# Delta-attention layer on one core: one VectorE multiply scales the a and q rows of a level, the query norm is folded into the output norm, and the queues are reordered

## What is computed

```python
q = _conv_silu(x @ Wq, conv_q).reshape(b, t, H, DH)
k = _conv_silu(x @ Wk, conv_k).reshape(b, t, H, DH)
v = _conv_silu(x @ Wv, conv_v).reshape(b, t, H, DH)
g_raw = (x @ Wfa @ Wfb).reshape(b, t, H, DH) + dt_bias.reshape(H, DH)
g = -jnp.exp(A_log)[None, None, :, None] * _softplus_stable(g_raw)
beta = jax.nn.sigmoid(x @ Wb)
qf = _l2norm(q) * DH ** (-0.5)
kf = _l2norm(k)
def step(state, inp):
    q_i, k_i, v_i, g_i, b_i = inp
    state = state * jnp.exp(g_i)[..., None]
    inner = jnp.einsum('bhk,bhkv->bhv', k_i, state)
    state = state + jnp.einsum('bhk,bhv->bhkv', b_i[..., None] * k_i, v_i - inner)
    o_i = jnp.einsum('bhk,bhkv->bhv', q_i, state)
    return (state, o_i)
...
rstd = jax.lax.rsqrt(jnp.mean(o * o, axis=-1, keepdims=True) + EPS)
o = o * rstd * norm_w * jax.nn.sigmoid(g_out)
return o.reshape(b, t, KD) @ Wo
```

## Time and profile before

| | |
|---|---|
| median of three runs | 6265.92 us |
| lowest and highest of them | 6243.98 and 6275.91 us |
| the profiled execution | 6272.03 us |
| its span, first to last instruction | 6270.3 us |
| the 32 passes in it | 2168 to 4352 us |
| TensorE's granted clock, whole span | 0.939 |
| TensorE's granted clock in the passes | 0.99 |

### The profile page before, as it was taken

How to read it: one execution, slowest core, us unless ns; L and a number is a source line. 1 busy time by engine, 2 the same in 40 slices (tenths; PEclk the granted TensorE clock), 3 DMA queues, 4 the chain that set the end, 5 groups by cost and what they waited for, 6 DMA issues and landing times. The chain is left out here.

```text
span 6270.3 us, 125078 instructions
## 1 busy us (share of the span) xinstructions
PE 5487.5 (88%) x53008; PEld 3632.2 (58%) x53008; DVE 3220.0 (51%) x4649; ACT 2789.8 (44%) x5107; POOL 2304.6 (37%) x1583
## 2 busy tenths in 40 slices
PE   6888699755999599989989989998999988889999
PEld 5777466543666266666666666665444456664444
DVE  5555444434444376776776677675212166552221
ACT  3233444454444456555655655665211166662111
POOL 4554100001000176777777677675222200002222
PEclk8999799877999799999999999999999988889999
DMA  0000100000000000000000000000211100002111
GB/s 29 3 2 2 33 1 1 16 0 33 1 1 3 22 17 23 18 17 23 18 17 17 24 17 17 23 18 9 107 40 40 34 11 0 0 1 108 39 40 46
DMA packets 60618, 137.02 MB, mean 22 GB/s; under 512 B 11638, under 2 KB 24054, under 8 KB 58842
## 3 DMA queue, kind: packets, MB, share of 16 engines
q1 hardware_dynamic: 60122, 129.79, 6.2%
HBM read 127.26 MB, written 2.50 MB: 21 GB/s over the span
## 5 line engine op out<-in xcount | busy, mean ns | idle before, releaser
L607 PE MATMUL ps<-moe_xn_all,moe_w 128*128 128x512 f32 x1792 | 810.5, 595 | 0.0
L720 DVE TENSOR_TENSOR moe_h<-moe_silu,ps 128x512 f32<-128x512 f32 x224 | 153.9, 687 | 936.2 <-ACT moe_silu L662 929.1
L607 PEld LDWEIGHTS ps<-moe_xn_all,moe_w 128*128 128x128 f32 x1792 | 341.2, 191 | 424.1 <-issue 423.5
L662 ACT ACTIVATE moe_silu<-ps 128x512 f32<-128x512 f32 x224 | 133.8, 597 | 986.5 <-PE ps L607 986.4
L1797 DVE SCALAR_TENSOR_TENSOR kda_cv<-kda_pre,kda_w_front,kda_cv 128x1024 f32<-128x1024 f32 x297 | 554.8, 1885 | 1.3
L563 POOL TENSOR_TENSOR moe_h<-moe_h,moe_cb 128x512 f32<-128x512 f32 x176 | 233.6, 1327 | 696.4 <-DVE moe_h L720 696.4
L1983 POOL TENSOR_TENSOR kda_g<-kda_g,kda_f 128x512 f32<-128x512 f32 x225 | 395.4, 1757 | 205.7 <-DVE kda_rows L1975 197.1
L617 PE MATMUL ps<-moe_h,moe_w 128*128 128x512 f32 x896 | 420.4, 592 | 0.0
L1681 PE MATMUL ps<-kda_xn_all,kda_w_front 128*128 128x512 f32 x808 | 373.6, 606 | 26.0 <-DMA kda_w_front<-in_Kw 23.5
L1975 POOL TENSOR_TENSOR kda_rows<-kda_q,kda_f 128x512 f32<-128x512 f32 x225 | 361.1, 1605 | 16.6 <-POOL kda_f L1984 1.6
L1984 POOL TENSOR_TENSOR kda_f<-kda_f 128x512 f32<-128x512 f32 x225 | 313.9, 1395 | 17.6
(11 more groups left out here) (505 smaller groups left out, 12513.3 us busy)
## 6 DMA issues: line engine op xcount, KB each, us to landing
kda_col<-kda_beta SPq DMA_DIRECT2D x34, 512.0 KB, 3.9
moe_w<-in_Mw SPq DMA_DIRECT2D x6, 2816.0 KB, 19.6
moe_cb<-kda_beta SPq DMA_DIRECT2D x64, 256.0 KB, 3.1
kda_w_front<-in_Kw SPq DMA_DIRECT2D x34, 455.0 KB, 4.7
moe_cb<-kda_beta SPq DMA_DIRECT2D x32, 224.0 KB, 2.9
kda_w_out<-in_Kw SPq DMA_DIRECT2D x32, 192.5 KB, 2.4
moe_cb<-kda_beta SPq DMA_DIRECT2D x32, 192.0 KB, 2.8
moe_cb<-kda_beta SPq DMA_DIRECT2D x32, 160.0 KB, 2.7
```

Source lines behind the costliest of these rows:

```text
L607: last = nc.tensor.matmul(ps_gu[u % 2][r], w13[:, k, i, r], n.xn[:, k, cols(c)], start=k == 0, stop=k == KD - 1)
```

## The change

It does the following.

- `q` and `a` lie in one tile `aq_rows`, and `scale_both` multiplies both halves by `f` in one VectorE instruction of 1024 elements for levels 1 to 6. GpSimd's q instruction of those levels goes. Level 0 stays on GpSimd.
- `widen` is cut in two: GpSimd widens the columns before it waits for the rows, and the rows behind that wait.
- The query is no longer normalised: `squares(0)`, `log_sum(0)`, `root(0)` and `q_row` go. ScalarE squares q into `q_sq` instead (`q_square`), and VectorE adds it, scaled, to the squares of the output (`with_query`), ahead of the tail's `square_sums`.
- TensorE does `scores(l + 1)` right behind `lt_times_t(l)`, ahead of `t_times_x(l)`; `values` moves from level 4 to behind level 5.
- On ScalarE and VectorE front and tail pieces are put at other places; the first tap of the next front (`first_tap`) is done at the end of a pass instead of behind its first rows.
- A table that nothing reads (`level_mask`, 128 by 448 floats) is no longer loaded at the start of the launch. `lt6` shares the memory of `z`.

```diff
-            def squares(i):
-                if i == 0:
-                    pe.wait_ge(m.vt_in_sb, at(m.vt_in_sb, 1))
-                else:
-                    pe.wait_ge(m.ss_read, at(m.ss_read, 1))
-                pe.wait_ge(m.sq_ready, at(m.sq_ready, i + 1))
+            def squares():
+                pe.wait_ge(m.proj_read, at(m.proj_read, 2))
+                pe.wait_ge(m.sq_ready, at(m.sq_ready, 1))
...
+            def q_square():
+                act.wait_ge(m.silu_ready, at(m.silu_ready, 1))
+                if in_chain:
+                    act.wait_ge(m.ysum_ready, at(m.ysum_ready, 1))
+                nc.scalar.activation(o.q_sq[:], o.q[:], ACT.Square).then_inc(m.qsq_ready, 1)
...
-            def q_row():
-                dve.wait_ge(m.rs_ready, at(m.rs_ready, 1))
-                nc.vector.scalar_tensor_tensor(o.q[:], o.q[:], float(KDA_HEAD) ** -0.5, t2[:], ALU.mult,
-                                               ALU.mult).then_inc(m.rows_ready, 1)
...
+            def with_query():
+                dve.wait_ge(n.ysq, at(n.ysq, 2))
+                if turn.index:
+                    dve.wait_ge(m.qsq_ready, at(m.qsq_ready, -1))
+                nc.vector.scalar_tensor_tensor(y_sq[:], o.q_sq[:], QUERY_EPS * KDA_HEAD, y_sq[:], ALU.mult,
+                                               ALU.add).then_inc(m.ysum_ready, 1)
...
+        def scale_both(o, l, done):
+            h = 1 << l
+            blocks = [P, 2, UNITS * SEQ // (2 * h), h]
+            out = rows_s[l % 2][:].rearrange("p r u (b h) -> p r (u b) h", h=h)
+            src = o.aq[:].rearrange("p r u (b two h) -> p r (u b) two h", two=2, h=h)[:, :, :, 1]
+            decay = halves(o.f[:], h, 1).unsqueeze(1).to_broadcast(blocks)
+            nc.vector.tensor_tensor(out, src, decay, ALU.mult).then_inc(done, 1)
...
         def first_rows(pool, step, o):
...
-            pool.wait_ge(m.rows_ready, at(m.rows_ready, 2))
-            for r in range(2):
-                scale_rows(nc.gpsimd, o, 0, r, n.first_scaled)
+            pool.wait_ge(m.rows_ready, at(m.rows_ready, 1))
+            scale_rows(nc.gpsimd, o, 0, 0, n.first_scaled)
             pool.wait_ge(n.g_clear, at(n.g_clear, 1))
+            widen_columns(step, o, 0)
+            pool.wait_ge(m.silu_ready, at(m.silu_ready, 3))
+            scale_rows(nc.gpsimd, o, 0, 1, n.first_scaled)
             pool.wait_ge(n.first_scaled, at(n.first_scaled, 2))
-            widen(step, o, 0)
+            widen_rows(step, o, 0)
...
-                scale_rows(nc.gpsimd, cur, l, 1, n.scaled)
                 nc.gpsimd.tensor_tensor(halves(cols_s[l % 2][:], h, 0), halves(cur.col[:], h, 0),
                                         halves(decay_g[:], h, 0), ALU.mult).then_inc(n.scaled, 1)
-                pool.wait_ge(n.scaled, at(n.scaled, 2 * l))
+                pool.wait_ge(n.scaled, at(n.scaled, l))
+                widen_columns(step, cur, l)
                 pool.wait_ge(n.rows_scaled, at(n.rows_scaled, l))
-                widen(step, cur, l)
+                widen_rows(step, cur, l)
...
+            lt_times_t(4)
+            scores(5)
+            t_times_x(4)
+            tail.y_of(1)
+            f.squares()
+            lt_times_t(5)
+            last_scores()
+            t_times_x(5)
+            f.values()
+            tail.square_sums()
             last_x()
-            pe.wait_ge(m.ss_read, at(m.ss_read, 2))
+            pe.wait_ge(m.vt_in_sb, at(m.vt_in_sb, 1))
             ahead.project(0)
```

More of the change, by code:

```diff
@@ L1847, in column @@
                                                ALU.mult).then_inc(m.rows_ready, 1)
-            return Calls(clip=clip, tap=tap, corr=corr, q_row=q_row, a_row=a_row, column=column)
+            return Calls(clip=clip, tap=tap, corr=corr, a_row=a_row, column=column)
         def tail_pe(pe, o, w, quad):
@@ L1968, in residual @@
                 nc.vector.tensor_tensor(xs, two(OUT[k]), xs, ALU.add).then_inc(n.x_done, 1)
[L1970 removed]
+            return Calls(inner=inner, right_side=right_side, gate=gate, with_query=with_query, scale=scale,
+                         residual=residual)
         def scale_rows(engine, o, l, r, done):
@@ L2179, in chain_act @@
                 nc.scalar.activation(aq[lower, mats(c), upper], ps_sc6[c][:, :, 1], ACT.Copy).then_inc(n.aq_in_sb, 1)
+            act.wait_ge(n.e1_in_sb, at(n.e1_in_sb, 1))
+            f.values()
+            tail.log()
             f.inverse()
             copy_x(B_LEVELS, upper)
+            f.root()
             tail.root()
-            f.root(0)
-            f.root(1)
             f.decays()
@@ L2261, in chain_dve @@
             tail.inner(0)
+            rows(2)
+            masks(1)
             f.clip()
-            masks(1)
-            a_rows(2)
-            f.tap(0, 1)
+            masks(2)
             f.tap(0, 2)
-            f.tap(1, 0)
             dve.wait_ge(n.t_ready, at(n.t_ready, 3))
             update(1)
+            rows(3)
             tail.gate(0)
+            f.tap(1, 0)
             f.tap(1, 1)
-            masks(2)
-            a_rows(3)
-            f.tap(1, 2)
-            f.tap(2, 0)
+            masks(3)
+            rows(4)
             update(2)
             tail.right_side()
-            masks(3)
-            a_rows(4)
+            f.tap(1, 2)
+            masks(4)
+            rows(5)
+            update(3)
+            tail.inner(1)
+            f.tap(2, 0)
+            masks(5)
+            rows(6)
+            update(4)
+            f.corr(0)
             f.tap(2, 1)
-            tail.inner(1)
-            update(3)
             f.tap(2, 2)
-            masks(4)
-            a_rows(5)
-            f.corr(0)
-            update(4)
+            tail.with_query()
             tail.gate(1)
-            masks(5)
-            a_rows(6)
+            last_masks()
             update(5)
-            last_masks()
             f.corr(1)
             f.corr(2)
+            f.a_row()
             tail.scale()
-            f.q_row()
-            f.a_row()
             f.column()
+            first_tap()
             tail.residual(0)
```

186 lines of the change are left out of this document (88 added, 98 removed).

## The result

| | before | after |
|---|---|---|
| median | 6269.41 us | 6083.49 us |
| lowest and highest of four runs | 6243.98 and 6275.91 us | 6073.35 and 6092.14 us |
| span of the profiled execution | 6270.3 us | 6071.5 us |
| the 32 passes, first gate to the 33rd | 2185.85 us | 2014.73 us |
| a pass, mean of 32 | 68.31 us | 62.96 us |

The change makes the kernel faster: the ratio is 0.971, with a 95% interval of 0.9677 to 0.9743.

The account below looks back on a forecast made before the run. The prediction took the port shared by VectorE and GpSimd, within a closed loop through the last tap, as the bound: five terms sum to 65.5 us, 65.0 taken; 6272.0 - 82 - 6 = 6184 us, range 6110 to 6248.

Parts of the forecast that it names:

- the port: VectorE instructions with two SBUF inputs and GpSimd multiplies go one at a time; the change saves 3.5 us a pass there.
- the masks: TensorE's `lt_times_t` waits for VectorE's masks, made late by the port: about 5.5 us a pass, falling to about 2.
- The pass it began from: A pass before the change, taken as 67.56 us from the distance of one group in two passes.
- The loop: Gate, rows, last tap of v, ScalarE to `inverse`, VectorE, GpSimd, `residual(0)`, next gate: 65.5 us, 65.0 taken.
- term 3: ScalarE from `silu(2)` to `inverse`, without a gap: 11.35 less overlap at eight joints, 11.0 us.
- Term 2: Rows of level 1 to the end of `tap(2,2)`: port work 41.3 us, at 98% full 42.1.
- Races: At levels 5 and 6 GpSimd's column multiply asks just ahead of a tap; otherwise 1.12 us each falls behind the last tap.
- The scaled rows: VectorE's six row scalings grow from 0.6 to 1.14 us each, +3.2 a pass; upper end 1.4, costing 1.5 more.
- the slower rival: Strided row scaling at 1.85 us instead of 1.14 makes `tap(2,2)` late: pass 69.2, 6318 us; chance 0.06.
- The ends: Outside the 32 passes: shorter block ahead, one more clear, `with_query` in the last tail; together -6 us.
- the floor: TensorE bounds the pass if VectorE and GpSimd run side by side: 61 us, 6058 in all; anything below 64.0 has 0.20.
- 62 to 64 by lucky turns: Part of the floor rival: a pass of 62 to 64 us by lucky turns at the port; anything below 64.0 has 0.20.

Follow-up runs that it names:

- the clear: Changed kernel with a GpSimd clear of the column tile before each column multiply of levels 1 to 6: 6142.62 us.
- the multiply: Changed kernel with GpSimd's column multiply of levels 1 to 6 done twice: 6329.04 us.
- `corr(0)` late: Changed kernel with VectorE's `corr(0)` moved from ahead of the last two taps to behind `update(5)`: 5993.47 us, again 6008.43 us, ratio 0.958 to the kernel before.
- the rows together in the old order: Kernel before, changed only so that one VectorE instruction scales both rows of levels 1 to 6 from one tile: 6196.45 us, ratio 0.988.
- the rows apart in the new one: Changed kernel with the q rows of levels 1 to 6 back on GpSimd: 6188.32 us, ratio 0.9854 to the kernel before.
- the copy first: Changed kernel with ScalarE's copy of x of level 5 ahead of `silu(2)`: 6064.07 us.
- both moves: Changed kernel with ScalarE's `copy_x(5)` ahead of `silu(2)` and `corr(0)` behind `update(5)`: 6024.42 us, ratio 0.9609 to the kernel before.

## Why the prediction was wrong, step by step

**What bounded it: right on the port, wrong on the masks.** In the changed kernel port turns set when the last tap ends (the clear against the multiply, and `corr(0)` late). That share was overrated: before, the stretch was not 98% full but, at the price found below, 94%, 31.2 of 33.2 us, and taking GpSimd's six multiplies away in the old order gave 0.86 of the 3.5 us a pass. And TensorE's waits for masks were not the port's in the main: they are 175 us before, 160 with the rows together in the old order, and 24 with the rows apart in the new one. Nor was there nothing to be won by the clock: 14 passes of before lose 1.5 us each to it.

**The pass it began from: wrong, 24 us.** 67.56 came from one distance between two groups. The mean is 68.31, and 0.75 x 32 = 24: the 14 passes of the longer kind, 1.5 each, a last one of 71.6 and a first one of 66.4. The pass ahead of the one it read is longer by 1.5; two distances in a row would have shown it.

**The loop, term by term.** The pass of after from 2848.34 is cut where the prediction cut it:

| term | forecast | measured |
|---|---|---|
| 1. gate to rows of level 1 | 1.4 | 1.20 |
| 2. to the end of the last tap | 42.1 | 39.3 |
| 3. `silu(2)` to the end of `inverse` | 11.0 | 10.7 |
| 4. `corr(1)` to the end of `a_row` | 3.6 | 3.6 |
| 5. the rest, to the gate | 7.4 | 7.4 |
| sum | 65.5 (65.0 taken) | 62.2 |

The rows of VectorE on which the cuts stand (timeline of after):

```profile
2849.54 1.23 DVE L2000 TENSOR_TENSOR kda_rows<-kda_aq_rows,kda_f 128x1024 f32<-128x1024 f32 x1
...
2899.59 1.23 DVE L1841 TENSOR_TENSOR kda_t<-kda_t,kda_v_in 128x1024 f32<-128x1024 f32 x1 [6.25 <-ACT kda_v_in L1787]
...
2903.19 1.22 DVE L1979 TENSOR_TENSOR kda_gated<-kda_gated,kda_y_sq 128x1024 f32<-128x1024 f32 x1
```

The last tap ends at 2884.57 + 4.28 = 2888.85, and the next gate starts at 2910.61. On ScalarE, the two ends of term 3:

```profile
2888.88 1.06 ACT L1754 ACTIVATE kda_v_in<-kda_cv 128x1024 f32<-128x1024 f32 x1 [3.75 <-DVE kda_cv L1803]
...
2898.50 1.06 ACT L1787 ACTIVATE kda_v_in<-kda_f 128x1024 f32<-128x1024 f32 x1
```

The loop is the right one: the four other terms came within some 0.3. With `corr(0)` late it still closes: the gate to the last tap 38.3, then 10.8, 3.6 and 7.4, 60.1 of a pass of 60.15.

**Term 2, the port's stretch, is the step that failed: 2.8 of the 3.2 us a pass by which the sum of 65.5 is too long, some 90 us in all.** Its count was right but for one instruction; the price of a turn was not.

- *Price.* The prediction took 1.12 for a GpSimd multiply, as at level 2, and 1.14 for a VectorE instruction. From 2873.85, where the multiply ahead of the fourth-last tap ends, to 2888.85 there are 14 of them in 15.0 us without a gap, 1.07 each (rows under Races). GpSimd's multiplies get shorter as the blocks grow. The widening of `g` that waits for the rows scaling takes 1.15 from the end of that scaling at level 2 and 0.92 at level 6 (VectorE, then GpSimd):

```profile
2857.37 1.21 DVE L2000 TENSOR_TENSOR kda_rows<-kda_aq_rows,kda_f 128x1024 f32<-128x1024 f32 x1
...
2881.33 1.32 DVE L2000 TENSOR_TENSOR kda_rows<-kda_aq_rows,kda_f 128x1024 f32<-128x1024 f32 x1
```

```profile
2857.47 2.26 POOL L2006 TENSOR_TENSOR kda_g<-kda_g,kda_f 128x512 f32<-128x512 f32 x1
...
2881.64 1.93 POOL L2006 TENSOR_TENSOR kda_g<-kda_g,kda_f 128x512 f32<-128x512 f32 x1
```

  With 34 instructions at 1.07, and the 0.6 and 1.2 of the prediction, the stretch comes to 38.2 of the 39.3 measured, 97%: nearly the fill that the prediction took. The price is worth some 2 us a pass.
- *Races.* GpSimd's `qf`, counted ahead of the last tap, fell behind it: its row begins at 2887.73, but the tap has the port until 2888.85. That is one turn, 1.1 us. The two races that the prediction named, at levels 5 and 6, both went to the tap, which asks before GpSimd's column multiply does (VectorE, then GpSimd); the first of these taps shows nearly its lone duration of 1.22:

```profile
2873.78 1.27 DVE L1803 SCALAR_TENSOR_TENSOR kda_cv<-kda_pre,kda_w_front,kda_cv 128x1024 f32<-128x1024 f32 x1
...
2879.02 1.42 DVE L1803 SCALAR_TENSOR_TENSOR kda_cv<-kda_pre,kda_w_front,kda_cv 128x1024 f32<-128x1024 f32 x1
```

```profile
2872.74 1.11 POOL L2012 TENSOR_TENSOR kda_f<-kda_f 128x512 f32<-128x512 f32 x1 [1.23 <-DVE kda_rows L2000]
2873.92 2.27 POOL L2035 TENSOR_TENSOR kda_cols<-kda_col,kda_g 128x512 f32<-128x512 f32 x1
...
2879.43 2.13 POOL L2035 TENSOR_TENSOR kda_cols<-kda_col,kda_g 128x512 f32<-128x512 f32 x1
```

  The prediction's sum for them is off as well: by its own 1.12 each, both make 63.3 and not 64.3, and even odds 64.4 and not 65.0.

**The scaled rows: right.** An instruction of 1024 with strided halves and a broadcast takes 1.23 alone (2849.54), as any two-input one does. The strided rate of the slower rival, 1.85, did not come.

**The waits it forecast: right in place, small in size.** Masks fell from 5.5 to 0.2 us a pass, where 2 were forecast; `t_times_x(5)` waits 1.29 instead of 2 to 3, in line with the tap that ends earlier; the gate waits 1.5, within 1 to 2.

**What took some back: 22 us.** The mean pass is 62.96, the plain one 62.27; 0.69 x 32 = 22. Of these 16 are the 12 stretches at the lower clock, which the forecast had at none, and 6 the first and the last pass. In all: -82 (forecast), -24 (base), -87 (62.27 for the 65.0 taken), +22 give -171, the difference of the two windows.

**The ends: 28 us where 6 were forecast, most of it not explained.** The block from its clears to the first gate takes 72.3 instead of 77.2, 4.9 less, against 7 forecast for it (-9.5, +1.5 and the clear's +1). The rest lies in parts that the change leaves as they were, but for the table no longer loaded: TensorE's first matmul comes at 9.87 instead of 10.59. Behind the last gate the two executions differ by 11 us, while the experiments took 1889 to 1921 us for that stretch; two experiments with the same code ahead of the first gate reached it at 2157.16 and 2166.89. A single pair of traces cannot tell 10 us there; the medians of the runs differ by 186 us, 15 more than the passes. With the ends at 22 more than forecast, the profiled execution lies 111 us below its forecast: -87, -24, -22 and +22.

**The rivals.** The time is that of the floor by its number, a pass below 64.0, and not by its reason: the engines still take turns (the busy 37.34 us of VectorE and 35.61 of GpSimd in 39.4 hold each other's turns as waits), and the taps end 40.5 us behind the gate, not 37. Of the slot "62 to 64 by lucky turns" one turn came, 1.1 us; the larger part, the price, is no luck of turns. The range went down to a pass of 62.7, and the mean pass of 62.96 lies inside it: what put the time below the range is the base and the ends. With the base right the range would have reached down to 6086, still 3 above the median.

**Left open.** Why the clock falls in some passes and not in others that idle at the same place was not settled. The same gap of 1.93 us stands ahead of a group at full and of one at half clock. What the runs do show is that the fall goes with TensorE's wait at level 5: with the rows apart the wait is 2.1 us and the clock falls there in 32 of 32 passes, with the clear 1.9 and 27, in the changed kernel 1.3 and 13, with the copy first 1.3 (ahead of `values`) and 7, and with `corr(0)` late there is neither. The kernel with the rows together in the old order, and the one with both moves, have such a stretch only at the end of the last pass. What the folded norm is worth without the new order was not run, nor the new order without the folded norm; nor which of the moves in the order freed the masks.

## What to carry to other kernels

Sum a closed loop through the engines rather than busy shares, and where two engines take turns count the instructions of both in one queue; then price each kind of instruction at the place and shape it has, not at the one place where it stood out. Measure a pass over several periods before subtracting from it: two kinds of passes can alternate under one mean clock. Where such a queue sets the end, find the one instruction that ends it and put behind it what doesn't feed it: moving `corr(0)` gave a further 2.1 us a pass, until the instruction that ended last was another.

## What the runs showed of the chip

- GpSimd's multiply of 512 elements by two SBUF inputs, timed from the end of the VectorE instruction it waits for, took 1.15 us at blocks of 4 tokens and 0.92 at blocks of 64.
- Fourteen VectorE and GpSimd instructions that read SBUF, each engine always with one queued, ran one at a time in strict turns: 15.0 us, 1.07 each.
- A GpSimd clear of 0.95 us ran beside a two-input tap of VectorE without lengthening it (1.09 us beside the clear, after the multiply's end).
- TensorE ran at half its clock in a part of some passes, and that cost 1.2 to 1.5 us there; passes with the same gap ahead of the same group did not have it, and the kernel with passes of 60.15 had it in none.
